# Rows kept in SBUF from the second gather pass to the MLP pass, and a list's ranks made one pass earlier

## What is computed

```python
def _layernorm(x, axis=-1, eps=1e-05):
    m = jnp.mean(x, axis=axis, keepdims=True)
    v = jnp.var(x, axis=axis, keepdims=True)
    return (x - m) / jnp.sqrt(v + eps)
```

## Time and profile before

| | us |
|---|---|
| Time, median of 3 runs | 6499.26 (6485.71 to 6501.09) |
| Profiled execution, its span | 6462.1 |
| PE busy | 3919.6 |
| POOL busy | 2886.1 |
| DVE busy | 2177.2 |
| ACT busy | 1422.3 |
| DMA moved | 692.13 MB, mean 107 GB/s |

### The profile page before, as it was taken

How to read it: one execution, slowest core, us unless ns; L and a number is a source line. 1 busy time by engine, 2 the same in 40 slices (tenths; PEclk the granted TensorE clock), 3 DMA queues, 4 the chain that set the end, 5 groups by cost and what they waited for, 6 DMA issues and landing times. The chain is left out here.

```text
span 6462.1 us, 74448 instructions
## 1 busy us (share of the span) xinstructions
PE 3919.6 (61%) x19983; PEld 3086.7 (48%) x19983; DVE 2177.2 (34%) x4653; ACT 1422.3 (22%) x3080; POOL 2886.1 (45%) x2799
## 2 busy tenths in 40 slices
PE   3333451668656742667466759888952669626697
PEld 2122121667422322666265646776732668426586
DVE  7444790324645620124311102343530112102134
ACT  0000000001333420112200126443420223302135
POOL 2555406663566766661555540000146660366602
PEclk8555575555666765555555569999975555755569
DMA  3000131111445641223734436554631222412235
GB/s 99 2 2 2 47 113 33 43 42 42 155 175 202 234 153 38 66 70 138 264 99 101 107 116 202 181 180 181 227 113 35 69 69 84 145 36 69 69 106 177
DMA packets 354959, 692.13 MB, mean 107 GB/s; under 512 B 183337, under 2 KB 185254, under 8 KB 339130
## 3 DMA queue, kind: packets, MB, share of 16 engines
q1 hardware_dynamic: 148381, 491.73, 21.7%
q10 hardware_dynamic: 118428, 130.12, 6.0%
q0 software_dynamic: 87808, 66.01, 5.8%
HBM read 350.87 MB, written 349.58 MB: 108 GB/s over the span
## 5 line engine op out<-in xcount | busy, mean ns | idle before, releaser
L1058 PE MATMUL e_ring<-e_msgs,e_hot 128*128 x6272 | 1419.4, 413 | 1091.3 <-issue 1082.7
L1058 PEld LDWEIGHTS e_ring<-e_msgs,e_hot 128*128 128x128 f32 x6272 | 1385.0, 328 | 1127.4 <-issue 1125.9
L925 POOL DMA_INDIRECT e_msgs<-y,index_D x784 | 741.4, 946 | 640.9 <-POOLq L77 261.1
L977 DVE TENSOR_TENSOR e_hot<-e_nodes,keys_D 128x2048 f32<-128x2048 f32 x147 | 336.9, 2292 | 1596.9 <-remote 872.0
L599 POOL DMA_INDIRECT list_D<-d_place,d_target x392 | 456.2, 1164 | 326.6 <-DVEq L553 210.5
L925 POOL DMA_INDIRECT e_msgs<-y,index_S x392 | 396.8, 1012 | 387.7 <-DVE index_S L963 198.3
L599 POOL DMA_INDIRECT list_S<-s_place,s_target x392 | 390.6, 996 | 362.8 <-DVEq L553 247.5
L1241 POOL DMA_INDIRECT m_far<-x,index_S x392 | 390.9, 997 | 347.9 <-DMA pairs_by_edge<-m_far 221.4
L1410 PE MATMUL m_ring<-m_region,m_hot 128*128 x1568 | 375.9, 426 | 215.7 <-issue 213.3
L925 POOL DMA_INDIRECT e_msgs<-x_by_relation,index_D x392 | 374.0, 954 | 210.4 <-issue 112.8
L1410 PEld LDWEIGHTS m_ring<-m_region,m_hot 128*128 128x128 f32 x1568 | 348.1, 328 | 244.3 <-issue 242.2
(11 more groups left out here) (368 smaller groups left out, 5846.1 us busy)
## 6 DMA issues: line engine op xcount, KB each, us to landing
x_by_relation<-d_stage SPq DMA_DIRECT2D x98, 1024.0 KB
agg<-e_stage ACTq DMA_DIRECT2D x196, 256.0 KB
n_in<-agg SPq DMA_DIRECT2D x42, 896.0 KB, 5.6
x<-n_out SPq DMA_DIRECT2D x28, 896.0 KB, 3.6
m_keyrow<-keys_by_step SPq DMA_DIRECT2D x49, 512.0 KB
m_region<-pairs_by_edge SPq DMA_DIRECT2D x49, 512.0 KB
messages<-m_region SPq DMA_DIRECT2D x98, 256.0 KB
m_region<-messages SPq DMA_DIRECT2D x49, 512.0 KB, 4.1
```

The lines of the kernel that those rows point to most:

```text
L925: pool.indirect_dma_start(out=msgs[:, (i % HELD) * D:(i % HELD + 1) * D], out_offset=None, in_=source, in_offset=bass.IndirectOffsetOnAxis ...
L977: nc.vector.tensor_tensor(hot[g % 2][:, :, :], bc(nodes[:, 0:P].unsqueeze(1), [P, GS, P]), bc(order["keys"][:, g * GS:(g + 1) * GS].unsque ...
L1058: mm = nc.tensor.matmul(ring[:, bass.ds(bucket, D)], hot[g % 2][:, k, :], msgs[:, bass.ds(tile, D)], start=False, stop=False, skip_group_c ...
```

## The change

It has three parts.

1. The table of rows lives in SBUF (`rows`, 128 x 25088 floats) from e1 to the end of the MLP pass. In e1 SP loads x1 into it in seven parts of 1.83 MB, one at a time, ahead of its loop of messages; banks are begun from it and carried out into it; after the last group the layernorm runs in the same pass, on the same arrays, and `x2` and `x2_turned` are stored from there. `agg1`, n2's pass and the MLP pass's loads of rows are gone. The scratch of e1's start lies in the last two parts of `rows`, which are loaded after it is used.
2. The ranks of 84 of D's 98 quads are made in e0, two quads in each of 42 groups (3 to 31 and 36 to 48): PE spreads the keys behind the group's steps, and DVE ranks them one group later, behind that group's go. The other 14 are ranked in the d pass's first 14 slots.
3. In the d pass a slot looks up two quads in place of one, so that all 98 are looked up in the first 49 slots; the target of unit u is made at slot 7(u+1)//2, and the one-hots two slots or so ahead of their use.

In the MLP pass, SP's first loads of keys stand in the common loop, and with them the spills that belong to groups 7 to 9.

The core of the diff:

```diff
-XCHUNKS = 7
+ROWPARTS = 7
+ROWS = T * D // ROWPARTS
+EARLY = 5
+RANKED_AGAIN = 36
+RANKED = tuple(range(3, 32)) + tuple(range(RANKED_AGAIN, GROUPS))
+EARLY_RANKS = 2 * len(RANKED)
+LOOKED = 2
...
     def dve_rank(self, dve, q, begin=0):
+        i = q - begin
+        of = self.p_k[i % len(self.p_k)]
+        dve.wait_ge(self.sem("spread"), i + 1)
...
+    def pe_keys(self, pe, q, begin=0):
+        i = q - begin
+        if i >= n:
+            pe.wait_ge(self.sem("rank"), i - n + 1)
```

On SP in `stair_pass`:

```diff
+            if rows is not None:
+                for c in range(ROWPARTS):
+                    if c == EARLY and fresh is not None:
+                        sp.wait_ge(s_keys, 2)
+                    if c >= 1:
+                        sp.wait_ge(s_rows, 16 * c)
+                    sp.dma_start(rows[:, c * ROWS:(c + 1) * ROWS], begin[:, c * ROWS:(c + 1) * ROWS]
+                                 ).then_inc(s_rows, 16)
             for b in range(BATCHES):
```

On DVE in `stair_pass`, in the loop of groups and behind it:

```diff
+                    for q in ranked.get(g - 1, ()):
+                        sort.dve_rank(dve, q)
...
+                for c in range(CHUNKS):
+                    h = c % 2
+                    x_c = nodes_of(rows[:, c * CW:(c + 1) * CW])
+                    dve.wait_ge(s_stage, CH * (c + 1))
+                    nc.vector.tensor_reduce(mean[h][:, :], x_c, AX.X, ALU.add).then_inc(s_sum, 1)
```

On PE in `stair_pass`, behind a group's steps:

```diff
                     if g == 33:
+                        pe.wait_ge(sort.sem("rank"), 2 * sum(r < 33 for r in RANKED))
                         sort.pe_steps(pe)
+                    if g == RANKED[0]:
+                        pe.wait_ge(s_keyt, 2)
+                    if g == RANKED_AGAIN:
+                        pe.wait_ge(sort.sem("steps"), 1)
+                    for q in ranked.get(g, ()):
+                        sort.pe_keys(pe, q)
```

On ACT in `stair_pass`, in `begin_bank`:

```diff
+                if rows is not None:
+                    act.wait_ge(s_rows, 16 * (b * 512 // ROWS + 1))
+                    nc.scalar.copy(ring[:, b % RING * 512:(b % RING + 1) * 512], rows[:, b * 512:(b + 1) * 512]
+                                   ).then_inc(s_free, 1)
+                    return
```

On SP in `mlp_pass`:

```diff
-            for c in range(XCHUNKS):
-                if c + 2 < XCHUNKS:
-                    load_rows(c + 2)
-                hand_rows(c)
-                load_keys(c + 3)
-            for g in range(XCHUNKS + 3, GROUPS):
+            for g in range(GROUPS):
                 load_keys(g)
                 while spills < (3 * g - 15) // 4:
                     spill(spills)
```

On DVE in `place_and_relate`:

```diff
-                    if c < CHUNKS:
-                        sort.dve_rank(dve, c * UQ + n)
-                    if n == 0 and 1 <= c <= CHUNKS:
-                        sort.dve_unit(dve, c - 1)
-                    if n == 2 and c + 1 < CHUNKS:
-                        hots(c + 1)
+                    if at in unit_at:
+                        sort.dve_unit(dve, unit_at[at], EARLY_RANKS)
+                    if EARLY_RANKS + at < QUADS:
+                        sort.dve_rank(dve, EARLY_RANKS + at, EARLY_RANKS)
+                    if at in hots_at:
+                        hots(hots_at[at])
```

On PE in `place_and_relate` (ACT's casts are doubled likewise):

```diff
+                    for q in range(LOOKED * at, LOOKED * (at + 1)):
+                        if q < QUADS:
+                            if q % UQ == 0:
+                                pe.wait_ge(sort.sem("onehot"), q // UQ + 1)
+                            sort.pe_hots(pe, q)
+                        if 1 <= q <= QUADS:
+                            sort.pe_lookup(pe, q - 1)
+                    if EARLY_RANKS + at < QUADS:
+                        sort.pe_keys(pe, EARLY_RANKS + at, EARLY_RANKS)
```

More of the change, by code:

```diff
@@ L532, in dve_unit @@
         m = 8 * u
-        dve.wait_ge(self.sem("rank"), UQ * (u + 1))
+        if UQ * (u + 1) > begin:
+            dve.wait_ge(self.sem("rank"), UQ * (u + 1) - begin)
         dve.wait_ge(self.sem("found"), UQ * (u + 1))
@@ L834, in stair_pass @@
 def stair_pass(nc, label, K, order, column, source, sums, fresh=None, sort=None, extra=None, turned=None,
-               start=None, scale=None):
+               start=None, scale=None, rows=None, normed=None):
     with ExitStack() as ctx:
@@ L857, in stair_pass @@
         hot = [sb(f"hot{h}", [P, GS, P]) for h in range(2)]
-        stage = [sb(f"stage{r}", [P, 512]) for r in range(RING)]
+        stage = [sb(f"stage{r}", [P, 512]) for r in range(RING)] if rows is None else None
         blank = sb("blank", [P, 512])
@@ L889, in stair_pass @@
             s_keys = sem("keys")
-        if start is not None:
+        if rows is not None:
+            s_rows = sem("rows")
+            s_begun = sem("begun")
+            begin = start.rearrange("(p t) f -> p (t f)", p=P)
+        elif start is not None:
             first = [sb(f"first{r}", [P, 512]) for r in range(RING)]
@@ L948, in _ @@
                 sp.wait_ge(s_turned, 16)
+            if normed is not None:
+                for c in range(CHUNKS + 1):
+                    if c < CHUNKS:
+                        sp.wait_ge(s_norm, c + 1)
+                        sp.dma_start(x_out[:, c * CW:(c + 1) * CW], rows[:, c * CW:(c + 1) * CW]).then_inc(s_xout, 16)
+                    if c >= 1:
+                        sp.wait_ge(s_turn, NQ * c)
+                        sp.dma_start(x_turned[:, (c - 1) * CW:c * CW], flat_t[(c - 1) % 2]
+                                     ).then_inc(s_tout[(c - 1) % 2], 16)
+                sp.wait_ge(s_xout, 16 * CHUNKS)
+                for h in range(2):
+                    sp.wait_ge(s_tout[h], 16 * (CHUNKS // 2))
         @block.vector
@@ L1090, in bank_out @@
                 r = m % RING
+                if rows is not None:
+                    held = rows[:, m * 512:(m + 1) * 512]
+                else:
+                    held = stage[r][:, :]
                 if scale is None:
-                    nc.scalar.copy(stage[r][:, :], ring[:, r * 512:(r + 1) * 512]).then_inc(s_stage, BL)
+                    nc.scalar.copy(held, ring[:, r * 512:(r + 1) * 512]).then_inc(s_stage, BL)
                     return
@@ L1122, in _ @@
                 act.wait_ge(s_group, done)
-                if m >= RING:
+                if m >= RING and rows is None:
                     act.wait_ge(s_store[r], 16 * (m // RING))
@@ L1130, in _ @@
                     begin_bank(m + RING)
+                if rows is not None:
+                    continue
                 act.dma_start(to[:, m * 512:(m + 1) * 512], stage[r][:, :]).then_inc(s_store[r], 16)
@@ L1192, in mlp_pass @@
         before = K["landed"]()
-        s_near = [sem(f"near{r}") for r in range(RING)]
         s_keyrow = [sem(f"keyrow{r}") for r in range(HOTS)]
```

214 lines of the change are left out of this document (155 added, 59 removed).

## The result

The changed kernel takes 6621.6 us (6601.33 to 6629.76) beside 6500.2 us for the kernel before: a ratio of 1.017, with a 95% interval of 1.0146 to 1.0195. It is slower, by 121 us where 6600 was forecast. The profiled execution has a span of 6628.0 us, 166 more than the 6462.1 of before.

The account below looks back on a forecast made before the run. No engine was taken to bound the whole; in the d pass all engines crawl beside POOL's unbroken puts. Span 6462.1 + 65 (d) + 50 (e0) + 5 (e1, norm) - 17 (mlp) = 6565, plus 37 to the median: 6600 us, range 6410 to 6690.

Parts of the forecast that it names:

- A: d pass: puts run without pauses, other engines crawl beside them, 60 slots left for after; 6600 us; chance 0.45.
- rival B: d pass: crawl belongs to slots with ranks, slots beside puts stay light, puts bound the pass; 6420 us; chance 0.27.
- C: d pass ends where it did, slots beside puts near 7.4 us; 6537 us in all; chance 0.15.
- E: d pass: two lookups make slots twice as long, POOL waits 60 us more; 6660 us, counted in A.
- the end of the puts: d pass: puts end at about 2180, POOL getting no long pause; 510 us of puts.
- The second term: d pass, after the last put: 60 slots remain at 3.8 us each, 228 us.
- the 14: e0's tail: PE's added rank matmuls, 13 groups at 1.1 us, 14 us.
- Rival D: e0: PE's added matmuls cost the crawl's price, +120, beside A; 6670 us; chance 0.13.
- the +15 for what of the loads shows: e1: SP's seven row loads take 43 us before a group may start, mostly hidden; +15, between 0 and +43.
- the 17 us: mlp: row loads gone (-9) and shorter stall on spills (-8), sum -17.
- the step from span to median: Whole kernel: runs' median stood 37 us above the profiled span, taking 6565 to 6602, given as 6600.
- upper bound of +125: d pass, slow side: POOL pauses 60 us more than in the +65 estimate; +125.

Follow-up runs that it names:

- e0: Not a run: a gather pass of the kernel, ahead of the d pass; its stage takes 696 us before the change and 732 us after.
- e4: Changed kernel plus a 1.8 us pause (POOL clears a spare tile) after every 16 puts of the d pass: 6446.1 us, ratio 0.9911 to the kernel before.
- e9: The changed kernel itself run again, beside a kernel before of 6439.2 us: 6560.7 us, ratio 1.021.
- e3: As a run: kernel before with only the rows kept in SBUF, one rank and one lookup a slot: 6465.9 us, ratio 0.9946 to before.
- e1: As a run: changed kernel with one lookup a slot again in the d pass; rows in SBUF and early ranks stay: 6446.2 us, ratio 0.9942 to before.
- e2: Changed kernel with all ranks back in the d pass, two a slot; two lookups and rows stay: 6673.2 us, ratio 1.0247 to the kernel before.
- e11: Changed kernel plus one 0.32 us clear after every 16 puts of the d pass, on a chip that crawls: 6554.0 us, ratio 1.0177 to before.
- e10: Changed kernel plus pauses of some 2 us after every 16 puts or gathers in all seven passes, crawling chip: 6244.5 us, ratio 0.9704 to before.
- e5: Changed kernel plus a 0.33 us break after every 16 puts of the d pass, chip without crawl: 5173.5 us, ratio 0.9971 to before (5185.6 us).

## Why the prediction was right

**The mechanism.** The likeliest case, A, came: the puts run in bursts without pauses, the rest crawls beside them, slots stay behind and run at the DMA's pace after the last put. e4 shows it by experiment: a pause after every 16 puts, with no work taken away, gives 182 of the pass's 826 us back. With two lookups a slot, rival B's condition (slots under 7.4 us beside puts) is met only with pauses (5.5 us on average in e4) and on the chip without a crawl; it gave a d stage of 534 to 614 us (an end at 2180 to 2260), and 610 came where nothing crawls, 644 with the pauses. C and E are not what happened either: POOL's waits within the pass are 74 us, not 60 more than before's 81. Of the signs given for A, two were missed by a little: these 74 us were to stay under 60, and the stretch behind the last put was to be over 200 us and is 192.

**The d pass was mis-sized, +128 for +65.** The term that failed is the end of the puts. I took 510 us for them, 392 x 1.27 and short pauses. They took 616: 392 x (1.082 + 0.30) = 542, as they are longer beside DVE than I allowed, and 74 of waits. "POOL gets no long pause" was wrong; the two do not settle near 10 us but tip, from slots of 4.5 to 6 us into slots of 43 and 73, until POOL runs dry. The mean came out as I had it by accident, 61 slots in 616 us, 10.1 each. The second term held: 51 slots were left, not 60, and took 192 us, 3.8 each as forecast (192/51). 106 more for the puts, 36 less for the slots behind them, and 7 less ahead of the first put (17 us where it was 24) make the missing 63. In e9 the puts took 598 us and the pass 788, so the same term is over there by less.

**e0, +36 for +50.** The tail's groups take 7.68 us where they took 6.83, + 0.85 where 1.1 was used; 12 of them are 10 us of the 14. The gathers take 606 us, 20 more than 586, where 33 was forecast. e3 against e1 gives the same (697 and 731), e2 (699) too, so the term stands at 34. Rival D's price was not paid.

**e1 and n2, -12 for +5.** SP's seven loads took the 43 us forecast, and the first mean follows the last group 10 us sooner. DVE's row and SP's in order of time:

```profile
2517.23 42.85 SPq L1019 DMA_DIRECT2D rows<-x  x7
...
3179.70 2.02 DVE L1134 TENSOR_REDUCE e_mean<-rows 128x28 f32<-128x1792 f32 x1 [11.36 <-PE e_ring L1185]
```

DVE waits 11.4 us there, not 21.8. The term that failed is the +15 for what of the loads shows: the fourth group's one-hots (L1075, L977 before) come 176.2 us after the stage's start where they came at 171.3, and the last group's at 649.0 in both. All of it hides under the first burst of gathers, in which PE does next to nothing anyway.

**mlp, +8 for -17.** The 9.7 us before the first step are gone, and POOL's first stall on spills is shorter:

```profile
3311.06 5.77 PE L1556 MATMUL m_ring<-m_blank 128*128 128x512 f32 x8 [7.69 <-DVE m_blank L1501]
3316.91 5.93 PE L1570 MATMUL m_ring<-rows,m_hot 128*128 x32
...
POOL m_far L1420 <- DMA pairs_by_edge<-m_far: 26.9, 2, 16.6
```

The step at 3316.9 follows the clearing at once, and the stalls are 26.9 us, the longest 16.6, for 44.0 and 31.5. Yet the gathers of the pass take 747 us, 19 more than before. In e1, e2, e3, e4, e9 and e11, with this same pass, the stage takes 1260, 1268, 1255, 1261, 1252 and 1253 us, so before's 1260 is within their spread: neither the 17 us nor a loss of 8 stands out of it. Beside e9, on a chip more like that of before's trace, the change is -8. Where the rest is given back stays open; the pauses in this pass gain 105 (e10), so it crawls, and a start 10 us sooner may meet the same crawl, which is argued and not shown.

**The sum.** The parts gave +103 and the trace +166. What brought the forecast near was the step from span to median: I added 37 us, as the traced execution of before lay below its runs, and for the kernel after that is -6. The two errors, 63 short and 43 over, cancel to 20. That the total came within 22 us is luck in this part. A reader should take from it that the sign and the mechanism were forecast, and the size of d was not: +128 lies just past even its upper bound of +125.

**The skill's rule.** GpSimd's SBUF interfaces are shared with VectorE (the Trainium skill, GPSIMD Engine Reference, 1. Specifications), and by that rule moving the ranks shortens no put. The mean put went from 1164 to 1082 ns in the changed kernel, but in e4 (1159) and on the chip without a crawl (e5, 1165) it is where it was, and in e2, with all ranks in the pass, it is 1070: the puts were shorter where more of DVE's work stood behind the last one (109 of its 311 us in the changed kernel), and not for the ranks. So far the traces agree with the rule. The s pass, which the prediction took for a sign of it at 996 ns, is a weaker one: in e5 its puts take 1106. That a drawn-out put keeps the others going, so that the sharing helps here, is the reading given at e1, and not shown.

## What to carry to other kernels

When one engine issues small DMAs back to back, look at what the others do beside it, by stretches: their pace may depend on how long the issues go on without a pause, and then making the issuer's inputs ready sooner can make the kernel slower. Price such an edit by the slots that are left over behind the last issue, and try a pause of some 2 us every 16 issues before moving any work. Run the kernel before on every chip: a gain or loss that hangs on the crawl can turn round on the next one (the pauses give 0.970 on one chip and 1.066 on another).

## What the runs showed of the hardware

- On three chips the kernel before took 6439 to 6503 us (medians), and on one 5186 us, with the same granted clock (0.50) in the gather stretches compared. Stages without indirect DMAs take the same on both (n3 362 to 364 us); parts with them take 20 to 31% less on the second (ahead of e0 661 for 959, e0 534 for 732, e1 with its norm 638 for 793, mlp 1011 for 1268).
- On the first kind, beside puts or gathers 1.26 to 1.30 us apart, PE, DVE and ACT do few instructions: 59 matmuls in 114 us of the d pass, 93 in 146 us of e1. Beside puts 1.58 us apart PE does 1172 in 300 us. A pause of 1.8 us in every 16 puts keeps it out of the d pass (e4), one of 0.33 us doesn't (e11), and in e0 and e1 2.2 us end it only in part (e10). On this kind PE's matmuls beside e1's gathers stand up to 2.80 us apart, and 526 of SP's 2070 semaphore operations take 0.65 to 0.75 us, where 0.02 is usual.
- On the second kind, PE does 518 matmuls in 165 us beside gathers 1.24 us apart, and no semaphore operation of SP takes 0.65 to 0.75 us (e5).
